# A GNN and expert layer on one core: the attention vectors of relations 2 to 7 folded into the weights by VectorE instead of TensorE, and the last tile's rows stored in two parts

## The reference, cut to what matters

```python
xn = layernorm(x)
feat_all = einsum('ni,rhid->rnhd', xn, conv_weights)         # 8 relations, 4 heads, 64 values each
el = sum(feat_all[type, src] * attn_l[type], -1)             # one number per edge and head
er = sum(feat_all[type, dst] * attn_r[type], -1)
alpha = softmax over the edges of one dst of leaky_relu(el + er, 0.2)
x = x + segment_sum(alpha * feat_all[type, src], dst) + h_bias
x = x + experts(layernorm(x))                                # top 2 of 8, 256 -> 1024 -> 256, GELU
```

## Time and profile before

| | us |
|---|---|
| runs before: median (lowest, highest) of 3 | 2175.03 (2172.45, 2175.23) |
| the profiled execution's own time | 2174.1 |
| its span, first to last instruction | 2172.0 |
| TensorE busy in the span | 1840.9 |
| VectorE busy | 1137.2 |
| ScalarE busy | 850.6 |
| GpSimd busy | 1140.9 |

### The profile page before, as it was taken

One profiled execution on the slowest core, in us unless ns is written; L12 is line 12 of the kernel. 1 busy time (PEld: TensorE's weight loads), 2 busy tenths in 40 slices (PEclk: granted clock), 3 DMA queues, 4 the chain that ended last, 5 costly groups with the idle time before them and its releaser, 6 DMA issues. The chain is left out here.

```text
span 2172.0 us, 38726 instructions
## 1 busy us (share of the span) xinstructions
PE 1840.9 (85%) x9090; PEld 1554.6 (72%) x9091; DVE 1137.2 (52%) x3066; ACT 850.6 (39%) x2220; POOL 1140.9 (53%) x1130
## 2 busy tenths in 40 slices
PE   7999867888888887988888888887552999999998
PEld 6888766766767776766766766676352888888887
DVE  4333145767666677767767676776773121212121
ACT  2222354444444454544544544542083222222222
POOL 4000177777777777777777777776056122222222
PEclk9999857788788798888888888887855999999999
DMA  6443344444444444444444444443144777777764
GB/s 222 167 188 143 142 112 110 112 114 112 110 113 110 111 112 112 112 113 109 112 113 110 112 112 110 112 108 97 44 161 150 233 218 234 222 224 223 227 217 130
DMA packets 120198, 308.99 MB, mean 142 GB/s; under 512 B 26951, under 2 KB 70855, under 8 KB 105828
## 3 DMA queue, kind: packets, MB, share of 16 engines
q0 software_dynamic: 60192, 149.24, 26.7%
q1 hardware_dynamic: 59844, 158.18, 21.3%
HBM read 250.66 MB, written 57.71 MB: 142 GB/s over the span
## 5 line engine op out<-in xcount | busy, mean ns | idle before, releaser
L716 POOL DMA_INDIRECT gath<-feats,idxT x996 | 951.7, 956 | 512.6 <-issue 295.0
L1014 PE MATMUL psP<-gath,hot 128*128 128x260 f32 x1992 | 614.1, 462 | 50.7 <-DVE gath L825 49.9
L1014 PEld LDWEIGHTS psP<-gath,hot 128*128 128x128 f32 x1992 | 435.0, 230 | 135.3 <-issue 47.7
L1001 PEld LDWEIGHTS psE<-er,hotT 128*128 128x128 f32 x1992 | 294.8, 227 | 122.4 <-issue 121.4
L1001 PE MATMUL psE<-er,hotT 128*128 x1992 | 309.1, 304 | 79.3 <-issue 37.7
L937 ACT COPY hotT<-psOT 128x512 f32<-128x512 f32 x249 | 144.9, 582 | 453.5 <-PE psOT L985 453.2
L927 ACT ACTIVATE hot<-cst,ndlT 128x128 f32<-128x128 f32 x996 | 317.5, 393 | 6.5 <-PEq L307 6.5
L834 DVE TENSOR_TENSOR acc<-acc,psP 128x260 f32 x498 | 210.2, 422 | 195.8 <-PE psP L1014 76.0
L1536 POOL DMA_INDIRECT out<-yrow,node x66 | 102.6, 1555 | 390.9 <-DVE yrow L1651 292.5
L825 DVE TENSOR_TENSOR gath<-gath,psA 128x1024 f32<-128x1024 f32 x249 | 301.1, 1219 | 9.9 <-ACT gath L957 2.5
L1606 ACT ACTIVATE hT<-psH,w1buf 128x256 f32<-128x256 f32 (+1 forms) x320 | 119.1, 434 | 352.2 <-PE psH L1566 352.2
(11 more groups left out here) (224 smaller groups left out, 1192.9 us busy)
## 6 DMA issues: line engine op xcount, KB each, us to landing
w1buf<-in_experts SPq DMA_DIRECT2D x40, 1030.0 KB, 7.8
w2buf<-in_experts SPq DMA_DIRECT2D x40, 1024.0 KB, 5.4
feats<-frow SPq DMA_DIRECT2D x30, 1040.0 KB, 4.0
gath<-feats,idxT POOLq DMA_INDIRECT x996
meta<-in_edges SPq DMA_DIRECT2D x464, 12.0 KB
xrow<-slots_x SPq DMA_DIRECT2D x26, 258.0 KB, 6.4
b_all<-in_b SPq DMA_DIRECT2D x40, 128.0 KB, 6.5
xs<-xb SPq DMA_DIRECT2D x5, 768.0 KB, 10.0
```

What stands on the lines that cost most here:

```text
L716: pool.indirect_dma_start(gath[:, r, u], None, feats, bass.IndirectOffsetOnAxis(ap=idxT[:, r, u:u + 1], axis=0)).then_inc(gath_in[r], 16)
L1001: ins = pe.matmul(psE[:, u * W % 512:u * W % 512 + W], hotT[:, j % 2, k * P:(k + 1) * P], tables[k // BLK], start=True, stop=True)
L1014: ins = pe.matmul(psP[:, bank(g, b, r), 0:FW], hot[:, r, u], gath[:, r, u], start=u % BLK == 0, stop=u % BLK == BLK - 1)
```

## The change

For relations 2 to 7 (pairs 1 to 3) VectorE computes the folded columns from the weights that are in SBUF anyway: a product of the pair's two relations with the attention rows (left and right, 1024 values per partition, the weight rows read twice by a broadcast) and a sum over each head's 64 columns, for both halves of the input dimension. The attention rows come as one row of 1024 values that is written to all 128 partitions (512 KB) in place of the pair's two `wt` transfers. Pair 0 is folded by TensorE as before. On VectorE, `logit_columns(1)` moves between `normalise(2)` and `normalise(3)`. The last tile's store is cut in two: relations 0 to 5 when its job before the last is evacuated, relations 6 and 7 at the end.

```diff
-                    for k in range(KD):
-                        sp.dma_start(wt[:, k, of], conv_t[k * P:(k + 1) * P, :].rearrange("p (r c) -> p r c", r=RELS)[:, of]).then_inc(
-                            wt_in[pair], 16)
+                    if pair == 0:
+                        for k in range(KD):
+                            sp.dma_start(wt[:, k], conv_t[k * P:(k + 1) * P, :].rearrange("p (r c) -> p r c", r=2)).then_inc(wt_in, 16)
+                    else:
+                        sp.dma_start(attn_all[:, pair - 1].rearrange("p r s c -> p (r s c)"),
+                                     attn_rows[pair - 1:pair, :].to_broadcast([P, 4 * D])).then_inc(rows_in[pair - 1], 16)
...
+                    if i == TILES - 1:
+                        early = LAST_JOB[i] - 1
+                        sp.wait_ge(copied_act, act_done(early))
+                        sp.wait_ge(copied_dve, dve_done(early))
+                        sp.dma_start(feats_tiles[i * P:(i + 1) * P, 0:(RELS - 2) * FW],
+                                     frow[:, i % LEAD, 0:RELS - 2].rearrange("p r w -> p (r w)")).then_inc(part_stored, 16)
...
                 def logit_columns(pair):
-                    dve.wait_ge(fold_ready, pair + 1)
+                    of = slice(2 * pair, 2 * pair + 2)
+                    dve.wait_ge(rows_in[pair - 1], 16)
+                    dve.wait_ge(w_in[pair], 16 * KD)
+                    if pair > 1:
+                        dve.wait_ge(w_ready, pair)
                     for k in range(KD):
-                        ins = dve.tensor_copy(wext[:, k, 2 * pair:2 * pair + 2, D:W],
-                                              psW[:, k * 64 + pair * 16:k * 64 + pair * 16 + 16].rearrange("p (r c) -> p r c", r=2))
+                        step(dve.tensor_tensor(product[:], wext[:, k, of, 0:D].unsqueeze(2).to_broadcast([P, 2, 2, D]),
+                                               attn_all[:, pair - 1], ALU.mult))
+                        ins = dve.tensor_reduce(wext[:, k, of, D:W].rearrange("p r (s h) -> p r s h", s=2),
+                                                product[:].rearrange("p r s (h c) -> p r s h c", h=HEADS), AX.X, ALU.add)
+                        if k < KD - 1:
+                            step(ins)
                     ins.then_inc(w_ready, 1)
...
-                logit_columns(0)
+                first_logit_columns()
                 normalise(2)
+                logit_columns(1)
                 normalise(3)
-                for pair in range(1, 4):
+                for pair in range(2, 4):
                     logit_columns(pair)
...
-                    if i == LEAD - 2 and pair < 3:
-                        fold(pair + 1)
```

More of the change, by code:

```diff
@@ L203, in index_columns, with node_stage @@
     return dve.tensor_scalar(sb["ndlT"][:, r], ps[:, P:2 * P:HEADS], -1.0, None, ALU.mult)
-def node_stage(nc, sb, x, conv, conv_t, attn, edges, numbers_dram, feats, slots_x, cst_dram, bias, xb_dram):
+def node_stage(nc, sb, x, conv, conv_t, attn, attn_rows, edges, numbers_dram, feats, slots_x, cst_dram, bias, xb_dram):
     with ExitStack() as ctx:
@@ L228, in node_stage @@
         wext = t("wext", [P, KD, RELS, W])
-        wt = t("wt", [P, KD, RELS, D])
+        wt = t("wt", [P, KD, 2, D])
         attn_c = t("attn_c", [P, KD, RELS * 2])
-        attn_d = t("attn_d", [P, KD, RELS * 2, HEADS])
+        attn_d = t("attn_d", [P, KD, 4, HEADS])
+        attn_all = t("attn_all", [P, 3, 2, 2, D])
+        product = t("product", [P, 2, 2, D])
         stats = t("stats", [P, TILES, 6])
@@ L258, in node_stage @@
         cst_in, attn_in, last_in = sem("cst_in"), sem("attn_in"), sem("last_in")
-        wt_in, w_in = [sem(f"wt_in{pair}") for pair in range(4)], [sem(f"w_in{pair}") for pair in range(4)]
+        wt_in, w_in = sem("wt_in"), [sem(f"w_in{pair}") for pair in range(4)]
+        rows_in = [sem(f"rows_in{pair}") for pair in range(1, 4)]
         x_in = [sem(f"x_in{b}") for b in range(len(BATCHES))]
@@ L264, in node_stage @@
         bias_in, xb_ready, xb_stored = sem("bias_in"), sem("xb_ready"), sem("xb_stored")
+        part_stored = sem("part_stored")
         pad_ready, acc_zero, slots_zero = sem("pad_ready"), sem("acc_zero"), sem("slots_zero")
@@ L331, in _ @@
                         sp.wait_ge(copied_dve, dve_done(LAST_JOB[i]))
-                    sp.dma_start(feats_tiles[i * P:(i + 1) * P, :],
-                                 frow[:, i % LEAD].rearrange("p r w -> p (r w)")).then_inc(row_stored[i % LEAD], 16)
+                    lo = RELS - 2 if i == TILES - 1 else 0
+                    sp.dma_start(feats_tiles[i * P:(i + 1) * P, lo * FW:],
+                                 frow[:, i % LEAD, lo:].rearrange("p r w -> p (r w)")).then_inc(row_stored[i % LEAD], 16)
                     if i == 2:
@@ L349, in _ @@
                         load_records(sp, sb, edges, meta[:, g % 2], g, meta_in[g], range(part * GB // 4, (part + 1) * GB // 4))
+                sp.wait_ge(part_stored, 16)
                 for q in range(LEAD):
@@ L429, in columns_of, with first_logit_columns @@
                     index_columns(dve, sb, psW, g)
-                def logit_columns(pair):
-                    dve.wait_ge(fold_ready, pair + 1)
-                    for k in range(KD):
-                        ins = dve.tensor_copy(wext[:, k, 2 * pair:2 * pair + 2, D:W],
-                                              psW[:, k * 64 + pair * 16:k * 64 + pair * 16 + 16].rearrange("p (r c) -> p r c", r=2))
+                def first_logit_columns():
+                    dve.wait_ge(fold_ready, 1)
+                    for k in range(KD):
+                        ins = dve.tensor_copy(wext[:, k, 0:2, D:W], psW[:, k * 16:k * 16 + 16].rearrange("p (r c) -> p r c", r=2))
+                    ins.then_inc(w_ready, 1)
+                def logit_columns(pair):
+                    of = slice(2 * pair, 2 * pair + 2)
[3 more added lines that the diff above has]
+                        dve.wait_ge(w_ready, pair)
+                    for k in range(KD):
+                        step(dve.tensor_tensor(product[:], wext[:, k, of, 0:D].unsqueeze(2).to_broadcast([P, 2, 2, D]),
[4 more added lines that the diff above has]
+                            step(ins)
                     ins.then_inc(w_ready, 1)
@@ L445, in _ @@
                 for k in range(KD):
-                    ins = dve.tensor_tensor(attn_d[:, k], attn_c[:, k].unsqueeze(2).to_broadcast([P, RELS * 2, HEADS]),
+                    ins = dve.tensor_tensor(attn_d[:, k], attn_c[:, k, 0:4].unsqueeze(2).to_broadcast([P, 4, HEADS]),
                                             cst[:, C_HEAD + k * HEADS:C_HEAD + (k + 1) * HEADS].unsqueeze(1).to_broadcast(
-                                                [P, RELS * 2, HEADS]), ALU.mult)
+                                                [P, 4, HEADS]), ALU.mult)
                 ins.then_inc(attn_ready, 1)
@@ L516, in turn, with fold @@
                     ins.then_inc(xT_ready, 1)
[L518 to L521, removed]
+                def fold():
+                    pe.wait_ge(wt_in, 16 * KD)
                     for k in range(KD):
-                        for r in (2 * pair, 2 * pair + 1):
-                            at = k * 64 + r * 2 * HEADS
+                        for r in range(2):
+                            at = k * 16 + r * 2 * HEADS
                             for c in range(KD):
@@ L544, in _ @@
                 pe.wait_ge(attn_ready, 1)
-                fold(0)
+                fold()
                 turn(0)
@@ L1679, in build @@
         }
-        node_stage(nc, sb, ins["x"], ins["conv"], ins["conv_t"], ins["attn"], ins["edges"], ins["numbers"], feats, slots_x,
+        node_stage(nc, sb, ins["x"], ins["conv"], ins["conv_t"], ins["attn"], ins["attn_rows"], ins["edges"], ins["numbers"], feats, slots_x,
                    ins["consts"], ins["bias"], xb)
@@ L1715 @@
         "conv": np.asarray(L0_gnn_conv_weights).transpose(2, 0, 1, 3).reshape(D, RELS * D),
-        "conv_t": np.asarray(L0_gnn_conv_weights).transpose(1, 3, 0, 2).reshape(D, RELS * D),
+        "conv_t": np.asarray(L0_gnn_conv_weights).transpose(1, 3, 0, 2).reshape(D, RELS * D)[:, 0:2 * D],
         "attn": np.stack([np.asarray(L0_gnn_attn_l).reshape(RELS, D), np.asarray(L0_gnn_attn_r).reshape(RELS, D)], 1).reshape(
             RELS * 2, D).T,
+        "attn_rows": np.stack([np.asarray(L0_gnn_attn_l).reshape(RELS, D), np.asarray(L0_gnn_attn_r).reshape(RELS, D)], 1)[2:].reshape(
+            3, 4 * D),
         "bias": np.asarray(L0_gnn_h_bias).reshape(1, D),
```

## The result

Over 14 runs each the changed kernel took 2168.56 us in the median (2165.92 to 2172.51), the kernel before 2173.39 (2171.25 to 2176.35): ratio 0.9976, 95% interval 0.9969 to 0.9983. That is 4.8 us faster, where 13.2 were forecast. The profiled execution took 2166.39 us, span 2164.6.

A forecast was written before the change was run, and what follows sets the result against it. The node stage, running alone with TensorE busy nearly without a gap, was taken to bound the kernel. Profiled 2174.1 - 11.4 (job 19) - 1.8 (last store) = 2160.9, as a median 2161.8 us; 8-in-10 range 2158 to 2174.

The forecast's parts named there:

- Part 1: Node stage, TensorE: folds 1 to 3 leave its chain, 3 x 1.70 = 5.1 us off; the first fold stays.
- Part 2: Node stage, VectorE: products and sums take 1.22 us each, every pair over 2 us early, costing TensorE nothing.
- Part 3: SP's DMA queue: three 512 KB broadcasts replace plain loads of the same bytes, delaying everything behind them by 1.5 us.
- d: Delay of everything behind the three broadcasts, GpSimd's start included: taken as 1.5 us, between -0.3 and 13.8.
- the bias's 86 GB/s: Best rate of the 1 KB bias row written to 128 partitions; at this rate the three broadcasts would delay 13.8 us.
- the race: Node stage: VectorE's small instructions of `norms(1)` against GpSimd's bias addition; forecast to get through if d exceeds 0.3.
- Part 4: Node stage: VectorE's small instructions precede GpSimd's additions, the hole before row 4 goes; gain at job 19 12.9 - d, 11.4 us.
- Part 5: Node stage's last store: six of eight relations issued 1.9 us earlier, 1.8 us less wait (1.0 to 2.0).
- A: The forecast itself: GpSimd starts after VectorE's small instructions; 2158.5 to 2169 us, likeliest 2161.8; chance 0.64.
- B: GpSimd starts by the time L159 does, row 4 comes at 51.2 as before; 2173 us; chance 0.18.
- C: Slow broadcast in the DMA queue, delay 13.8 us, job 19 starts at 65.6; 2177 us; chance 0.12.
- D: VectorE's products take twice as long, tile 4 starts at 71 instead of 59.0; 2185 us; chance 0.06.

The follow-up runs named there:

- the kernel with the new order: Changed kernel, GpSimd's additions waiting for the small instructions of `norms(1)`, and the 16 statistics of `norms(2)` moved ahead of `normalise(5)`: 2162.61 us, ratio 0.9937 to before.
- the later occasion: The changed kernel itself, unedited, profiled and timed again beside the kernel before: 2172.17 us against 2174.74, ratio 0.9983.

## Why the prediction was wrong, by its steps

**Part 1, the folds**: right. From the start of job 1 to that of job 10 TensorE takes 16.24 us (16.36 to 32.60) instead of 21.61 (16.79 to 38.40), 5.4 us less where 5.1 were forecast, and nothing but a transpose stands between the jobs.

**Part 2, the products**: right. Six products and six sums of 1.22 us each; pair 3 is ready at 27.95, and its first job (job 9) starts near 30.6, by the pace of the nine jobs from 16.36 to 32.38. TensorE never waits for `w_ready`.

**Part 3, the transfers**: the term d was mis-sized. I took +1.5; GpSimd started at 32.11 and 32.14 in the two profiles of the changed kernel instead of 32.69, so d = -0.6. Whether that is outside the bound of -0.3 is not shown, since the start scatters: it was 31.67 in a profile of the kernel before with the split store,

```profile
31.67 16.73 POOL L370 TENSOR_TENSOR x_biased<-x_rows,bias_all 128x1024 f32<-128x1024 f32 x3 [24.34 <-DMA bias_all<-in_bias]
```

and 32.36 and 32.53 in two others with the transfers of before. In six profiles with the broadcasts it was 31.57 to 32.14. So the broadcasts cost no time that shows, and the bias's 86 GB/s was no guide to them. By itself this would have lost the race, for I had L161 start at 32.9. VectorE was early too, by 0.9 us (31.96), and a matter of 0.15 us was left.

**Part 4 is the step that failed.** I wrote that `normalise(4)` and `(5)` "end at 39.2". They are TENSOR_SCALAR with one input from SBUF, and I took the hold for one of instructions with two inputs, because the rows of before show only such instructions meeting GpSimd: there, L162 and L386 came when it was done. The runs show a TENSOR_SCALAR held just as long: 2.32 us (L162), 8.94 us (`normalise(5)`). It is not a matter of the mean and the scale that `normalise` reads beside its input, since L162 reads a constant there. What it costs follows from the order: `normalise(5)` ends at 49.0 instead of 39.2, the 16 statistics begin there instead of at 39.2, and job 19 starts at 56.44 where the sum gives 51.2 (51.8 + d, with d = -0.6; TensorE alone would be there at 51.0), and at half clock. That is 5.2 + 1.9 = 7.1 us in the case of the race won; the kernel with the new order gets them back (first gather 7.4 us sooner, times 7.5 us).

With that the sum closes for the profile with the race won: 12.9 + 0.6 for the folds and the wait, + 1.8 for the store, less 7.1 for the hold is 8.2, and 8.25 was measured at the first gather. So the forecast of 13.2 had two errors of opposite sign, 7.1 us too much for the hold that it left out and 2.1 too little for d. That the median has 4.8 and not 8.2 is only in part explained: a lost race takes 3 us (one profile), and the first gather in the profile of before is later by up to 1.9 us than two others of its kind say; how much either is in the median stays open.

The page of the Trainium skill that I cited ("SBUF — State Buffer", section "Who interferes with whom") also says that `tensor_scalar` can enter a mode with two ports and then contends with GpSimd. I used its sentence on two inputs and passed over this one, which spoke against the forecast. The trace agrees with it in the hold (8.94 us); whether the instruction was in such a mode no run here shows. What the page says of `tensor_reduce` was not put to the test in the node stage: the last of the six sums ended at 27.95, ahead of GpSimd's first addition. BATCH_NORM_STATS2 is another instruction; it kept its pace beside GpSimd (5.31 us for 16) in every profile where they met.

**Part 5, the store**: right, 1.8 forecast, 1.77 measured in the pair of profiles and 1.7 alone; SyncE's wait for the landing fell from 3.6 to 1.7 us, as the forecast had it.

**The rivals.** The two profiles of the changed kernel are neither A nor B. With the race won, the gain at the gathers is 8.2 us (A said 13.2); with it lost after L160, 5.2 us (B said 2, for a loss by L159). In the median it is 4.8, and 2.6 on the later occasion. The slow broadcast of C and the slow products of D did not occur. That 2168.56 lies inside the range, and even inside A's own of 2158.5 to 2169, is luck: A reaches it only with GpSimd 6 us late and the half clock back, and GpSimd was early. (A's lower end was also set too low: at d = -0.3 the sum gives 2160.0.)

## What to carry to other kernels

Where GpSimd works on SBUF beside VectorE, count its instructions by length, not by sum: a long one can hold VectorE for its whole length, up to 8.9 us here, and that goes for a simple one-input TENSOR_SCALAR as for a TENSOR_TENSOR with two inputs from SBUF. Here 30 pieces of 0.73 us cost less than 3 of up to 8.9 us although they add up to more. When a step is moved earlier, list everything that then falls into such a stretch, and ask of each instruction whether a row shows it beside such an addition; if no row does, both answers belong in the sum. And take more than one profile of the kernel before when the forecast hangs on some tenths of a microsecond: GpSimd's start moved by 1.0 us between profiles with the same transfers.

The best version here is the changed kernel with the additions in 30 instructions: 2159.35 us, ratio 0.9929 to the kernel before. The times don't tell it from the one with the race won and the new order (0.9937, 0.9923 to 0.9950).

## What the runs showed of the hardware that was not expected

- A TENSOR_SCALAR of 128x256 float32 takes 0.41 us alone, no faster than a BATCH_NORM_STATS2 of the same width (0.41), and yet took 8.94 us beside GpSimd's longest addition. A RECIPROCAL of 10 elements beside the addition ahead of that one took 0.22 us: it was not held.
- Between two additions that follow each other without a pause, one held instruction gets through, and sometimes a second. In the profile of before L158 took its usual 0.16 us behind L157; in one with the split store it took 8.88 us, to the end of the third addition.
- Three rows of 4 KB, each written to 128 partitions, cost the queue no time against plain loads of the same bytes: with them among the loads it moved 330 to 358 GB/s from 9.0 to 10.5 us. One row of 1 KB to 128 partitions, with nothing but small transfers beside it, moved at 86 to 90.
- On one of the three occasions of the experiments the gathers ran at 84 to 86 instead of 111 to 112 GB/s in every kernel that was profiled, which made the program 400 us longer and its times too scattered to tell a few us; the node stage was the same there to about a microsecond. Each occasion ran on another chip (numbers 9, 10 and 6; the slow one is 10), so whether it was the chip or the hour is open.
